# Four of the seven layer-0 tiles as three products of rounded parts and rests, and the diagonals on ScalarE

## The chip, the cores and the metric

The kernel runs on one core of a Trainium2 chip. The metric is the device time of one execution in microseconds (us), as the median of several runs. The core has five engines with queues of their own: TensorE (PE; its weight loads are shown apart, as PEld), VectorE (DVE), ScalarE (ACT), GpSimd (POOL) and SyncE (SP), which here only issues DMAs. The engines run their own instructions in order and wait for each other by semaphores.

## The reference

A recommendation tower: 39 embedding rows of 16 numbers for each of 512 samples, three layers of pairwise products with learned filters (a compressed interaction network), and three dense layers behind them.

```python
e = jnp.stack([tbl_f[ids[:, f]] for f in range(39)], axis=1)      # 512 x 39 x 16
x0 = xk = e
for W in (f0, f1, f2):                                            # 1521 x 128, 4992 x 128, 4992 x 128
    z = jnp.einsum('bfd,bgd->bfgd', x0, xk).reshape(b, f * g, d)
    cur = jnp.einsum('bpd,pm->bmd', z, W)                         # 512 x 128 x 16
    outs.append(cur); xk = cur
z = jnp.sum(jnp.concatenate(outs, axis=1), axis=-1)               # 512 x 384
h = jnp.maximum(jnp.concatenate([z, dense_ctx], axis=1) @ W_top1 + b_top1, 0.0)
h = jnp.maximum(h @ W_top2 + b_top2, 0.0)
y = h @ W_top3
```

## The kernel before

The batch is cut into 16 chunks of 32 samples, 512 columns (sample, dimension) each. Chunk 0 has its layer 0 in two halves; `i` counts these parts (part i is chunk i - 1 from i = 2 on).

Layer 0 of a part: because both factors are x0, pairs (f, g) are folded into 20 shifts, three shifts in a tile of 117 rows, seven tiles `t`. SyncE loads `x0_thrice` and, for each t, `shifted`; VectorE multiplies them into `z0` (`products0`, L525 to L538, the product at L537), which has three slots; TensorE multiplies z0 by `w0` in full fp32 and adds all seven tiles in the PSUM bank `acc0` (`layer0`, matmul at L755, two matmul records each). ScalarE then rounds acc0 to `x1_hi` (fp32r, `high_x1`, L631) and VectorE takes the rest `x1_lo` (`low_x1`, L545) and sums acc0 into `out0` (`sum_x1`, L550).

Layer 1 of a chunk: 40 strips (four sub-chunks `s` of 128 columns, ten strips `g` of up to four fields; the tenth has three). `layer1` makes each strip in three fp32r matmuls of up to 512 columns (L795 hi by hi, L796 hi by lo, L799 lo by hi) into one of seven PSUM banks. Each strip is scaled by x0 out of its bank: strips 0, 3, 5 and 8 of a sub-chunk by ScalarE (L687), strips 1, 2, 4, 6, 7 and 9 by VectorE (`scale`, L582, one instruction for a field). GpSimd adds ScalarE's products (L477) and VectorE's sums (L484, L487, L493) into `x2_t`, and between them issues the gathers of the embedding rows two chunks ahead (L467).

The order is written out by hand. Every engine walks the same loop over chunks c and places n = 0 to 39, one place for one strip, and the lists at the head of the file say at which place each other step stands; at a place these steps come ahead of the strip's own work. During chunk c, layer 0 of chunk c + 1 is made: `PRODUCT0_AT` has the places of VectorE's seven products, `LAYER0_AT` those of TensorE's seven tiles, `X1_AT` = (35, 36, 38) those of high_x1, low_x1 and sum_x1. The `_LATE_` lists hold for chunk 0 and for the chunks 4, 8 and 12, which close a quarter of the batch and carry layer 2 of that quarter (39 fp32 products, L827, at the places 13 to 20). TensorE turns x0 at place 6 (L764), and from chunk 1 on it makes at place 9 the sums of layer 2 of the chunk before (`sum_products`, L813), which take `x2_t` and the diagonals `x0_diag`. The diagonals are one VectorE instruction at place 20 (`diagonal`, L557).

The sums take four of the seven banks. The banks are handed out in turn, and a strip waits in `drained` until the slot seven before its own has been emptied. In a chunk from 1 on the strips 0 to 8 have the slots 0 to 8 of that chunk, the sums 9 to 12, strip 9 has 13, and strip 10 has 14. So the strip of place 9 waits for strip 6, that of place 10 for strip 7, that of place 11 for strip 8, and those from place 16 on for the strip seven before.

## Time and profile before

| what | value |
|---|---|
| median of 3 runs | 654.74 us (654.56 to 655.45) |
| the profiled execution | 655.72 us, of it 653.8 us span |
| PE busy | 623.2 us, 95% |
| PE weight loads busy | 468.0 us, 72% |
| DVE busy | 525.0 us, 80% |
| ACT busy | 337.7 us, 52% |
| POOL busy | 501.8 us, 77% |
| DMA engines, mean | 66 GB/s |
| chain that ended last, by engine | PE 90%, DMA 3%, DVE 2% |

The span is the time from the first to the last instruction in the trace; 1.9 us lie around it. Busy time is the time in which at least one instruction of an engine was under way, so instructions that overlap are counted once, while the mean duration of one counts each in full. Matmuls are pipelined: a 512-column matmul is recorded with 0.39 us, but in the chain of work the next one follows after 0.23 us, and that is its cost. The granted clock of TensorE is given as a share of full speed (2.4 GHz).

### The profile page before, as it was taken

The page shows a single profiled execution, that of the slowest core. Times are in us where ns is not written, and L with a number is a line of the kernel's source. Part 1 is how long each engine was busy: PE and PEld are TensorE (multiplying, and loading weights), DVE is VectorE, ACT ScalarE, POOL GpSimd, SP SyncE. Part 2 cuts the span into 40 slices and gives each one's busy share as a digit, 9 for nine tenths or more (in the row PEclk, how much of TensorE's full clock was granted, in tenths as well). Part 3 has the DMA queues.
Part 4 walks back from the last instruction along what each step waited for, and adds up shares of the span by engine and source line. Part 5 has one row for each costly group of instructions (what it writes and reads, how often), then busy time and mean ns, then how long its engine had stood idle before and what let it go on. Part 6 is the DMA issues. An engine that isn't in the chain of part 4 may idle for free.

```text
span 653.8 us, 10942 instructions
## 1 busy us (share of the span) xinstructions
PE 623.2 (95%) x3102; PEld 468.0 (72%) x3102; DVE 525.0 (80%) x1651; ACT 337.7 (52%) x1148; POOL 501.8 (77%) x486
## 2 busy tenths in 40 slices
PE   0599999999999999999999999999999999999998
PEld 0476777777796777777787777777787777778763
DVE  4499989989857898989867798989876798988800
ACT  3153646465543646565553556555553555557602
POOL 6789989898957889898975888898985786566710
PEclk9999999999999999999999999999999999999999
DMA  6464038231305013140404014040403104000000
GB/s 225 97 169 124 15 85 293 43 93 28 109 4 131 4 30 106 12 125 8 128 4 117 18 11 126 8 128 3 133 4 96 39 6 129 1 1 2 1 1 0
DMA packets 59014, 43.40 MB, mean 66 GB/s; under 512 B 37648, under 2 KB 42926, under 8 KB 58826
## 3 DMA queue, kind: packets, MB, share of 16 engines
q1 hardware_dynamic: 52854, 38.00, 20.0%
q0 software_dynamic: 5120, 1.32, 2.5%
q10 hardware_dynamic: 980, 3.39, 1.5%
q8 instruction: 24, 0.39, 0.3%
q14 instruction: 36, 0.29, 0.1%
HBM read 40.75 MB, written 1.94 MB: 65 GB/s over the span
## 4 chain that ended last, share of the span: by engine, by line
PE 90%; DMA 3%; DVE 2%; POOL 1%; SPq 1%; issue 1%; ACT 1%; POOLq 0%; DVEq 0%; ACTq 0%
PE strip L795 22%; PE strip L799 21%; PE strip L796 21%; PE acc L755 14%; PE acc L827 4%; PE strip L813 2%; DVE scaled L582 1%; PE strip L827 1%; PE strip L893 1%; PE acc L764 1%; DVE z L537 1%; DMA found<-in_tables,rows 1%; ACT first L687 1%; POOL found L467 1%; DMA shifted<-x_fields 0%
## 5 line engine op out<-in xcount | busy, mean ns | idle before, releaser
L582 DVE SCALAR_TENSOR_TENSOR scaled<-strip,x_t,scaled 128x128 f32<-128x128 f32 x1216 | 331.8, 340 | 26.8 <-PE strip L799 25.8
L795 PE MATMUL strip<-w_hi,x_hi 128*128 128x512 f32 (+1 forms) x640 | 298.3, 466 | 0.8 <-ACT x_hi L631 0.7
L799 PE MATMUL strip<-w_hi,x_lo 128*128 128x512 f32 (+1 forms) x640 | 248.9, 389 | 0.0
L796 PE MATMUL strip<-w_lo,x_hi 128*128 128x512 f32 (+1 forms) x640 | 248.4, 388 | 0.0
L477 POOL TENSOR_TENSOR added<-added,product 128x512 f32<-128x512 f32 x128 | 171.2, 1338 | 74.3 <-ACT product L687 71.3
L687 ACT ACTIVATE product<-strip,x_t 128x128 f32<-128x128 f32 x512 | 146.6, 372 | 144.1 <-PE strip L799 144.1
L467 POOL DMA_INDIRECT found<-in_tables,rows x160 | 160.7, 1004 | 28.5 <-issue 10.9
L795 PEld LDWEIGHTS strip<-w_hi,x_hi 128*128 128x128 f32 x640 | 120.2, 188 | 49.0 <-issue 15.0
L796 PEld LDWEIGHTS strip<-w_lo,x_hi 128*128 128x128 f32 x640 | 120.5, 188 | 44.9 <-issue 25.3
L799 PEld LDWEIGHTS strip<-w_hi,x_lo 128*128 128x128 f32 x640 | 120.1, 188 | 25.7
L687 ACT ACTIVATE added<-strip,x_t 128x128 f32<-128x128 f32 x256 | 73.0, 367 | 91.7 <-PE strip L799 91.7
L755 PE MATMUL acc<-z,w 117*128 117x512 f32 (+1 forms) x238 | 117.0, 577 | 3.2 <-ACT out L663 2.6
L582 DVE SCALAR_TENSOR_TENSOR scaled<-strip,x_t,first 128x128 f32<-128x128 f32 x256 | 71.8, 341 | 47.5 <-PE strip L799 25.0
L537 DVE TENSOR_TENSOR z<-shifted,x_thrice 117x512 f32<-117x512 f32 (+1 forms) x119 | 100.9, 850 | 10.9 <-DMA shifted<-x_half_fields 6.3
L484 POOL TENSOR_TENSOR added<-added,scaled 128x512 f32<-128x512 f32 x64 | 83.2, 1300 | 5.8 <-DVE scaled L582 2.9
L687 ACT ACTIVATE first<-strip,x_t 128x128 f32<-128x128 f32 x256 | 72.9, 367 | 27.5 <-PE strip L799 23.8
L755 PEld LDWEIGHTS acc<-z,w 117*128 117x128 f32 x238 | 45.1, 194 | 15.0 <-issue 4.3
L487 POOL TENSOR_TENSOR added<-added 128x256 f32<-128x256 f32 x64 | 51.4, 803 | 5.0
L493 POOL TENSOR_TENSOR x_t<-added 128x128 f32<-128x128 f32 x64 | 34.9, 545 | 5.0
L827 PEld LDWEIGHTS acc<-g_sum,w 128*128 128x128 f32 x234 | 29.8, 191 | 1.9
L827 PE MATMUL acc<-g_sum,w 128*128 128x128 f32 x234 | 30.0, 274 | 0.0
L654 ACT COPY g_sum<-strip 128x320 f32<-128x320 f32 (+2 forms) x68 | 24.4, 459 | 6.0 <-PE strip L813 6.0
(57 smaller groups left out, 181.7 us busy)
## 6 DMA issues: line engine op xcount, KB each, us to landing
shifted<-x_fields SPq DMA_DIRECT2D x105, 234.0 KB
x_thrice<-x_fields SPq DMA_DIRECT2D x15, 234.0 KB
found<-in_tables,rows POOLq DMA_INDIRECT x160, 5.0
w<-in_L_rec_f SPq DMA_DIRECT2D x1, 2496.0 KB, 10.4
g_sum<-in_L_rec_f ACTq DMA_DIRECT2D x4, 512.0 KB, 7.9
shifted<-x_half_fields SPq DMA_DIRECT2D x14, 117.0 KB
x_once<-x_fields SPq DMA_DIRECT2D x15, 78.0 KB
x_fields<-found SPq DMA_DIRECT2D x15, 72.0 KB
```

The source lines that it names most:

```text
L467: pool.indirect_dma_start(out=found[:, c % E_SLOTS, k, :], out_offset=None, in_=a["tables"][:, :], in_offset=bass.IndirectOffsetOnAxis(ap= ...
L477: pool.tensor_tensor(added[:, u % 2, :, :], added[:, u % 2, :, :], product[:, product_slot(u, k) % PRODUCTS, :, :], ALU.add).then_inc(add_ ...
L484: pool.tensor_tensor(added[:, u % 2, :, :], added[:, u % 2, :, :], scaled[:, u % 2, :, :], ALU.add).then_inc(add_step, 1)
L487: pool.tensor_tensor(added[:, u % 2, 0:2, :], added[:, u % 2, 0:2, :], added[:, u % 2, 2:4, :], ALU.add).then_inc(sum_step, 1)
L537: dve.tensor_tensor(z0[:, (T0 * i + t) % Z_SLOTS, columns], shifted[0:ROWS, t, columns], x0_thrice[:, p, columns], ALU.mult).then_inc(z0_r ...
L582: dve.scalar_tensor_tensor(into, strip[:, slot_of_strip(q) % Y_BANKS, j, :], x0_t[:, c % 2, s, f:f + 1], onto, ALU.mult, ALU.add).then_inc ...
L687: last = act.activation(into[:, j, :], strip[:, slot_of_strip(q) % Y_BANKS, j, :], ACT.Copy, scale=x0_t[:, c % 2, s, f:f + 1])
L755: pe.matmul(acc0[:, columns_of(i)], w0[:, t, :], z0[:, (T0 * i + t) % Z_SLOTS, columns_of(i)], start=(t == 0), stop=(t == T0 - 1)).then_in ...
L795: pe.matmul(into, x1_hi[:, c % 2, columns], hi, start=True, stop=False)
L796: pe.matmul(into, x1_hi[:, c % 2, columns], lo, start=False, stop=False)
L799: pe.matmul(into, x1_lo[:, c % 2, columns], hi, start=False, stop=True).then_inc(strip_ready, 1)
L827: last = pe.matmul(acc2[quarter], w2[:, f, :], g_sum[:, f, :], start=(f == 0), stop=(f == FIELDS - 1))
```

## The change

From chunk 2 on (parts i > 2, `in_three`), the last four tiles of layer 0 (t = 3 to 6) are no longer one fp32 product but three fp32r products: rounded w0 by rounded z0, rest of w0 by rounded z0, rounded w0 by rest of z0. The rounded part `z0_hi` is made by ScalarE (`high_z0`), the rest `z0_lo` by VectorE (`low_z0`); the parts of w0 are made once at the start. `z0` has a slot for each of its seven tiles instead of three in all. VectorE's products stand earlier: at the places 4, 5, 6, 7, 9, 11 and 13 instead of 6, 9, 12, 15, 18, 21 and 24, and in the late chunks at 8, 9, 10, 11, 13, 15 and 17 instead of 16 to 28; chunk 0 keeps its places. The rounded parts are made at 12, 14, 16 and 18, the rests at 13, 16, 19 and 22 (late: 16 to 22 and 18 to 27). The places of TensorE's tiles stay. The diagonals move from VectorE at place 20 to ScalarE at place 26, in two instructions instead of one. Left out below are only the declarations of the new tiles w0_hi and w0_lo and of the semaphores.

```diff
--- before.py
+++ after.py
@@ -105,7 +105,10 @@
 
 W1_PIECE = 8
 W1_PIECES = -(-FIELDS // W1_PIECE)
-Z_SLOTS = 3
+
+
+THREE = 4
+THREE_FROM = T0 - THREE
 
 
 
@@ -113,9 +116,14 @@
 DENSE_IN = 5
 DENSE_AT = 9
 KEEP_DENSE_AT = 10
-PRODUCT0_AT = [6, 9, 12, 15, 18, 21, 24]
+PRODUCT0_AT = [4, 5, 6, 7, 9, 11, 13]
+HIGH0_AT = [12, 14, 16, 18]
+LOW0_AT = [13, 16, 19, 22]
 LAYER0_AT = [12, 15, 18, 21, 24, 27, 30]
-PRODUCT0_LATE_AT = [16, 18, 20, 22, 24, 26, 28]
+PRODUCT0_FIRST_AT = [16, 18, 20, 22, 24, 26, 28]
+PRODUCT0_LATE_AT = [8, 9, 10, 11, 13, 15, 17]
+HIGH0_LATE_AT = [16, 18, 20, 22]
+LOW0_LATE_AT = [18, 21, 24, 27]
 LAYER0_LATE_AT = [22, 24, 26, 28, 30, 32, 34]
 TURN_X0_AT = (6, 8)
 X1_AT = (35, 36, 38)
@@ -125,7 +133,7 @@
 
 TURN_X0_LATE_AT = (17, 18)
 X1_HALF_AT = (13, 14, 15)
-DIAGONAL_AT = 20
+DIAGONAL_AT = 26
 LAYER2_AT = range(13, 21)
 LAYER2_STEP = 5
 KEEP_OUT1_AT = 12
@@ -170,6 +178,23 @@
     return c > 0 and c % PER_QUARTER == 0
 
 
+def in_three(i, t):
+
+    return i > HALVES and t >= THREE_FROM
+
+
+def three_before(i, t):
+    return THREE * (i - HALVES - 1) + t - THREE_FROM
+
+
+def parts0_at(c):
+
+    if c == 0 or c + 1 == CHUNKS:
+        return None, [], []
+    late = closes_quarter(c)
+    return part_of(c + 1, 0), HIGH0_LATE_AT if late else HIGH0_AT, LOW0_LATE_AT if late else LOW0_AT
+
+
 def layer0_at(c):
 
 
@@ -178,7 +203,8 @@
         plans.append((1, PRODUCT0_HALF_AT, LAYER0_HALF_AT, *TURN_X0_HALF_AT, *X1_HALF_AT))
     if c + 1 < CHUNKS:
         late = c == 0 or closes_quarter(c)
-        plans.append((part_of(c + 1, 0), PRODUCT0_LATE_AT if late else PRODUCT0_AT,
+        product_at = PRODUCT0_LATE_AT if c else PRODUCT0_FIRST_AT
+        plans.append((part_of(c + 1, 0), product_at if late else PRODUCT0_AT,
                       LAYER0_LATE_AT if late else LAYER0_AT,
                       *(TURN_X0_AT if c else TURN_X0_LATE_AT), *X1_AT))
     return plans
...
@@ -213,7 +241,9 @@
         x0_thrice = sb("x0_thrice", [ROWS, 2, N])
         x0_once = sb("x0_once", [P, 2, N])
         shifted = sb("shifted", [P, T0, N])
-        z0 = sb("z0", [ROWS, Z_SLOTS, N])
+        z0 = sb("z0", [ROWS, T0, N])
+        z0_hi = sb("z0_hi", [ROWS, THREE, N], F32R)
+        z0_lo = sb("z0_lo", [ROWS, THREE, N], F32R)
         x1_hi = sb("x1_hi", [MAPS, 2, N], F32R)
         x1_lo = sb("x1_lo", [MAPS, 2, N], F32R)
 
...
@@ -533,9 +567,21 @@
                     dve.wait_ge(thrice_in[p], 16 * arrivals(i))
                 dve.wait_ge(shifted_in[t], 16 * (i + 1))
 
-                at_least(dve, l0_step, T0 * i + t - Z_SLOTS + 1)
-                dve.tensor_tensor(z0[:, (T0 * i + t) % Z_SLOTS, columns], shifted[0:ROWS, t, columns],
+                if in_three(i - 1, t):
+                    dve.wait_ge(z0_lo_ready, three_before(i - 1, t) + 1)
+                else:
+                    at_least(dve, l0_step, T0 * (i - 1) + t + 1 if i else 0)
+                dve.tensor_tensor(z0[:, t, columns], shifted[0:ROWS, t, columns],
                                   x0_thrice[:, p, columns], ALU.mult).then_inc(z0_ready, 1)
+
+            def low_z0(i, t):
+                k = three_before(i, t)
+                dve.wait_ge(z0_hi_ready, k + 1)
+
+                if in_three(i - 1, t):
+                    dve.wait_ge(l0_step, T0 * (i - 1) + t + 1)
+                dve.tensor_tensor(z0_lo[:, t - THREE_FROM, :], z0[:, t, :], z0_hi[:, t - THREE_FROM, :].bitcast(F32),
+                                  ALU.subtract).then_inc(z0_lo_ready, 1)
 
             def low_x1(i):
                 p, columns = chunk_of(i) % 2, columns_of(i)
@@ -549,16 +595,6 @@
 
                 dve.tensor_reduce(out0[:, batch_of(i)], acc0[:, columns_of(i)].rearrange("m (b d) -> m b d", d=D),
                                   AX_X, ALU.add).then_inc(out0_ready, 1)
-
-            def diagonal(c):
-                dve.wait_ge(x0_t_ready, part_of(c, SUBS - 1) + 1)
-
-                at_least(dve, g_ready, c)
-                dve.tensor_tensor(
-                    x0_diag[:, :, :, 0:FIELDS],
-                    x0_t[:, c % 2, :, :].rearrange("p s (o f) -> p s o f", o=1).to_broadcast([P, SUBS, TILE_B, FIELDS]),
-                    mask[:].rearrange("p (a b o) -> p a b o", a=1, o=1).to_broadcast([P, SUBS, TILE_B, FIELDS]),
-                    ALU.mult).then_inc(diag_ready, 1)
 
             def scale(c, s, g):
 
@@ -592,6 +628,9 @@
                             .to_broadcast([P, SUBS, TILE_B])).then_inc(mask_set, 1)
             dve.wait_ge(w0_in, 32)
             dve.tensor_tensor(w0[:], w0[:], w0_mirror, ALU.add).then_inc(w0_ready, 1)
+            dve.wait_ge(w0_hi_ready, 1)
+            dve.tensor_tensor(w0_lo[:], w0[:, THREE_FROM:T0, :], w0_hi[:].bitcast(F32),
+                              ALU.subtract).then_inc(w0_lo_ready, 1)
 
             def low_w1(i):
                 of = w1_fields(i)
@@ -617,13 +656,31 @@
                             low_x1(i)
                         if n == sum_at:
                             sum_x1(i)
-                    if n == DIAGONAL_AT:
-                        diagonal(c)
+                    i, _, low_at = parts0_at(c)
+                    if n in low_at:
+                        low_z0(i, THREE_FROM + low_at.index(n))
                     if g in BY_DVE[s]:
                         scale(c, s, g)
 
         @block.scalar
         def _(act):
+            def high_z0(i, t):
+                act.wait_ge(z0_ready, T0 * i + t + 1)
+
+                if in_three(i - 1, t):
+                    act.wait_ge(l0_step, T0 * (i - 1) + t + 1)
+                act.copy(z0_hi[:, t - THREE_FROM, :], z0[:, t, :]).then_inc(z0_hi_ready, 1)
+
+            def diagonal(c):
+                act.wait_ge(x0_t_ready, part_of(c, SUBS - 1) + 1)
+                act.wait_ge(mask_in, 16)
+
+                at_least(act, g_ready, c)
+                for b in range(TILE_B):
+                    last = act.activation(x0_diag[:, :, b, 0:FIELDS], x0_t[:, c % 2, :, :], ACT.Copy,
+                                          scale=mask[:, b:b + 1])
+                last.then_inc(diag_ready, 1)
+
             def high_x1(i):
 
                 at_least(act, strip_ready, SLOTS * (chunk_of(i) - 1))
@@ -634,7 +691,6 @@
                 c, subs = chunk_of(i), subs_of(i)
 
                 at_least(act, scale_step, scaled_before(SUBS * (c - 1), 0) if c else 0)
-                at_least(act, diag_ready, c - 1)
                 act.wait_ge(x0_t_turned, i + 1)
                 act.copy(x0_t[:, c % 2, subs[0]:subs[-1] + 1, :],
                          x0_t_bank[i > 0][:, subs[0]:subs[-1] + 1, 0:FIELDS]).then_inc(x0_t_ready, 1)
@@ -694,6 +750,8 @@
             act.dma_start(w0_mirror, a["w0_lower"]).then_inc(w0_in, 16)
             for i in range(W1_PIECES):
                 act.dma_start(w1_raw[:, w1_fields(i), :], a["L0_rec_f1"][:, w1_fields(i), :]).then_inc(w1_in[i], 16)
+            act.wait_ge(w0_ready, 1)
+            act.copy(w0_hi[:], w0[:, THREE_FROM:T0, :]).then_inc(w0_hi_ready, 1)
             for i in range(W1_PIECES):
                 act.wait_ge(w1_in[i], 16)
                 act.copy(w1_hi[:, w1_fields(i), :], w1_raw[:, w1_fields(i), :]).then_inc(w1_hi_ready, 1)
@@ -714,6 +772,11 @@
                             high_x1(i)
                         if n == keep_at:
                             keep_x0_t(i)
+                    i, high_at, _ = parts0_at(c)
+                    if n in high_at:
+                        high_z0(i, THREE_FROM + high_at.index(n))
+                    if n == DIAGONAL_AT:
+                        diagonal(c)
                     if c and n == SUMS_AT:
                         keep_g(c - 1)
                     if c == CHUNKS - 1 and n == LAST_SUMS_AT:
@@ -741,7 +804,10 @@
         def _(pe):
             def layer0(i, t):
                 c = chunk_of(i)
-                pe.wait_ge(z0_ready, T0 * i + t + 1)
+                if in_three(i, t):
+                    pe.wait_ge(z0_lo_ready, three_before(i, t) + 1)
+                else:
+                    pe.wait_ge(z0_ready, T0 * i + t + 1)
                 if t == 0:
                     if i:
 
@@ -752,8 +818,15 @@
                     at_least(pe, out0_ready, i)
                     if closes_quarter(c - 1):
                         pe.wait_ge(out2_ready, (c - 1) // PER_QUARTER)
-                pe.matmul(acc0[:, columns_of(i)], w0[:, t, :], z0[:, (T0 * i + t) % Z_SLOTS, columns_of(i)],
-                          start=(t == 0), stop=(t == T0 - 1)).then_inc(l0_step, 1)
+                if in_three(i, t):
+                    k = t - THREE_FROM
+                    pe.matmul(acc0[:], w0_hi[:, k, :], z0_hi[:, k, :], start=False, stop=False)
+                    pe.matmul(acc0[:], w0_lo[:, k, :], z0_hi[:, k, :], start=False, stop=False)
+                    pe.matmul(acc0[:], w0_hi[:, k, :], z0_lo[:, k, :], start=False, stop=(t == T0 - 1)
+                              ).then_inc(l0_step, 1)
+                else:
+                    pe.matmul(acc0[:, columns_of(i)], w0[:, t, :], z0[:, t, columns_of(i)],
+                              start=(t == 0), stop=(t == T0 - 1)).then_inc(l0_step, 1)
 
             def turn_x0(i):
                 c = chunk_of(i)
@@ -835,6 +908,7 @@
             for t in range(T0):
                 layer0(0, t)
             pe.wait_ge(mask_set, 1)
+            pe.wait_ge(w0_lo_ready, 1)
             pe.wait_ge(x0_t_ready, 1)
 
             for c in range(CHUNKS):
```

## Rows read from the trace of the kernel before

**Rows 1.** Windows: span, PE, PEld, DVE, ACT, POOL busy (count); clock, DMA share, GB/s.
```profile
295.64:330.75 35.11, 35.11 (x175) 26.27 (x174) 32.71 (x105) 20.20 (x70) 31.26 (x31) 1.00 0.24 64
330.75:375.49 44.74, 43.87 (x252) 34.95 (x252) 31.24 (x103) 20.61 (x72) 30.89 (x31) 1.00 0.20 50
```

**Rows 2.** Chain of work that ended last, around place 9: start, duration, what.
```profile
295.64 1.06 PE strip L813 x32
296.70 0.38 PE strip L795
297.08 0.17 PE strip L796
297.25 0.18 PE strip L799
297.43 0.41 PE strip L795
297.84 0.23 PE strip L796
...
299.00 0.86 PE acc L755 x2
```

**Rows 3.** Waits between 74 and 600 us: total, times, longest.
```profile
PEld strip L795 <- DVE scaled L582: 12.7, 52, 0.4
```

**Rows 4.** Timeline of VectorE ahead of that place: start, duration, instruction, count.
```profile
292.42 2.15 DVE L582 SCALAR_TENSOR_TENSOR scaled<-strip,x_t,scaled 128x128 f32<-128x128 f32 x8
294.48 0.73 DVE L537 TENSOR_TENSOR z<-shifted,x_thrice 117x512 f32<-117x512 f32 x1
295.14 2.15 DVE L582 SCALAR_TENSOR_TENSOR scaled<-strip,x_t,scaled 128x128 f32<-128x128 f32 x8
297.21 2.14 DVE L537 TENSOR_TENSOR z<-shifted,x_thrice 117x512 f32<-117x512 f32 x1
299.28 0.86 DVE L582 SCALAR_TENSOR_TENSOR scaled<-strip,x_t,scaled 128x128 f32<-128x128 f32 x3
```

**Rows 5.** Groups of instructions by shape: busy, mean ns of one | idle before.
```profile
L537 DVE TENSOR_TENSOR z<-shifted,x_thrice 117x512 f32<-117x512 f32 x105 | 95.2, 907 | 3.6 <-PE acc L755 3.5
L557 DVE TENSOR_TENSOR x_diag<-x_t,mask 128x312 f32<-128x312 f32 x16 | 16.6, 1037 | 0.0
L631 ACT CAST x_hi<-acc 128x512 fp32r<-128x512 f32 x15 | 9.0, 602 | 0.1
```

**Rows 6.** Timeline of GpSimd over the same stretch.
```profile
293.39 0.74 POOL L487 TENSOR_TENSOR added<-added 128x256 f32<-128x256 f32 x1
294.21 0.46 POOL L493 TENSOR_TENSOR x_t<-added 128x128 f32<-128x128 f32 x1
294.62 1.74 POOL L477 TENSOR_TENSOR added<-added,product 128x512 f32<-128x512 f32 x1
296.51 0.96 POOL L467 DMA_INDIRECT found<-in_tables,rows  x1
297.49 1.31 POOL L477 TENSOR_TENSOR added<-added,product 128x512 f32<-128x512 f32 x1
```

**Rows 7.** Timeline of VectorE at the end of the chunk (idle before in brackets).
```profile
319.34 1.13 DVE L582 SCALAR_TENSOR_TENSOR scaled<-strip,x_t,first 128x128 f32<-128x128 f32 x4 [2.11 <-PE strip L799]
```

**Rows 8.** First chunk after a late one: VectorE's product at place 9, TensorE's chain.
```profile
225.97 0.68 DVE L537 TENSOR_TENSOR z<-shifted,x_thrice 117x512 f32<-117x512 f32 x1
226.27 0.38 PE strip L795
376.69 0.68 DVE L537 TENSOR_TENSOR z<-shifted,x_thrice 117x512 f32<-117x512 f32 x1
376.55 0.38 PE strip L795
```

**Rows 9.** Chain of work in part 0 and chunk 0.
```profile
26.64 0.42 DVE z L537
52.74 0.39 DVE x_diag L557
```

**Rows 10.** DMA queue of SyncE: last loads of one part, in the chunk ahead of its products.
```profile
313.58 5.80 SPq L420 DMA_DIRECT2D shifted<-x_fields  x7
```

**Rows 11.** TensorE idle near the end (idle before in brackets), and that window.
```profile
623.17 0.46 PE L813 MATMUL strip<-x_diag,x_t 32*128 32x80 f32 x8 [1.50 <-POOL x_t L493]
619.00:626.00 7.00, 5.50 (x31) 3.06 (x30) 0.14 (x1) 1.02 (x6) 3.70 (x4) 1.00 0.01 2
```

More of the change, by code:

```diff
@@ L204, in build_program @@
         w0 = sb("w0", [ROWS, T0, MAPS])
+        w0_hi = sb("w0_hi", [ROWS, THREE, MAPS], F32R)
+        w0_lo = sb("w0_lo", [ROWS, THREE, MAPS], F32R)
         w1_hi = sb("w1_hi", [P, FIELDS, MAPS], F32R)
@@ L281, in build_program @@
         w0_ready = sem("w0_ready")
+        w0_hi_ready = sem("w0_hi_ready")
+        w0_lo_ready = sem("w0_lo_ready")
         w1_hi_ready = sem("w1_hi_ready")
@@ L288, in build_program @@
         z0_ready = sem("z0_ready")
+        z0_hi_ready = sem("z0_hi_ready")
+        z0_lo_ready = sem("z0_lo_ready")
         l0_step = sem("l0_step")
```

## The prediction

> **What bounds the kernel now.** I read the views in this order: busy time in windows from one place 9 to the next, the chain of work that ended last, the waits, and then the timelines of the two engines that meet where the chain has its only irregular pieces.
>
> An ordinary chunk takes 35.11 us, and TensorE is busy for all of it; VectorE is busy for 32.71 us, so it has 2.4 us to spare, GpSimd 31.26 and ScalarE 20.20 us [rows 1]. A chunk that closes a quarter takes 44.74 us with VectorE at 31.24. TensorE sets the pace, and whatever shortens its own work shortens the chunk, as long as nobody makes it wait. That is where the reader should look twice. In the chain around place 9 the pieces of 512 columns follow each other every 0.23 us, but the first matmul of the strip at place 10 stands with 0.41 us [rows 2]: 0.18 us of waiting. The cause is VectorE: strip 10 may only start when the bank of strip 7 is empty, and VectorE ends strip 7 at 297.21, where its next instruction starts, 0.22 us before TensorE starts strip 10 at 297.43 [rows 2, 4]. The same piece, 0.36 to 0.48 us long, stands in 8 of the 11 ordinary chunks from chunk 1 to 14 (chunks 1, 2, 3, 6, 7, 10, 11, 14); in all, weight loads of strips waited for VectorE 52 times, most of them hidden behind the running matmul [rows 3]. So at the end of strip 7 VectorE has no slack, although it has 2.4 us over the whole chunk. Four of seven banks go to the sums at place 9, and the lead of TensorE over VectorE shrinks to three strips there.
>
> **TensorE's products.** An fp32 tile costs 0.86 us in the chain, an fp32r matmul of 512 columns 0.23 (three of them, from 297.84 on, take 0.70) [rows 2]. Per tile 0.86 - 0.70 = 0.16 us are saved; four tiles in 14 parts make 56 tiles, 56 x 0.163 = 9.1 us. Weight loads go from two to three a tile and fit under a matmul, as those of the strips do. TensorE never waits longer for z0_lo: a rest stands at least seven places ahead of its tile (13 to 21, 16 to 24, 19 to 27, 22 to 30; late 18 to 28 down to 27 to 34), and TensorE can't be more than seven strips ahead of VectorE.
>
> [...]
>
> **VectorE over the chunk.** Added are four rests a chunk, the same shape and the same two SBUF inputs as a product. A product has a mean of 0.907 us, 0.83 without the 0.08 in which neighbours overlap; removed is the diagonal, 1.04 - 0.08 = 0.96 [rows 5]. Per ordinary chunk 4 x 0.83 - 0.96 = +2.4 us, so VectorE needs some 32.8 + 2.4 = 35.2 us: about the old length of the chunk, just above the new length of TensorE's work (35.11 - 0.65 = 34.5).
>
> **VectorE up to strip 7: the step that decides.** Before, one product (place 6) stood ahead of the scaling of strip 7. Now four do: places 4, 5, 6 and 7, and strips 4, 6 and 7 are scaled between them. Strips 9 and 10 of TensorE wait for strips 6 and 7, so the three added products fall on the path. What each costs depends on GpSimd. Where GpSimd is in one of its additions, the product ends some 0.5 us after it: the product at 297.21 took 2.14 us, to 299.28, because the addition from 297.49 lasted to 298.80 [rows 4, 6]; undisturbed it takes 0.60 (0.68 recorded).
>
> I walk VectorE in the chunk of rows 4. Strips 2 and 4 take 2.06 us, so strip 2 ends at 293.45. Product 0 finds L487 running until 294.13 and ends at 294.60; strip 4 ends at 295.63; product 1 finds L477, shifted to about 295.2 to 296.5, and ends at 296.97; product 2 meets the gather, which doesn't hold it, and ends at 297.57; strip 6 at 298.60; product 3 finds the second L477 and ends at 299.42; strip 7 at 300.45. That is 3.2 us later than 297.21. If GpSimd's chain comes 0.6 us earlier (it has more time in a longer chunk), the same walk gives 299.8, 2.6 us later. With no conflict at all it is 293.45 + 4 x 0.60 + 3 x 1.03 = 298.94, 1.7 us later; with all four products held, about 3.8. I take S = 2.8 between the two walks, with ends 1.7 and 3.8.
>
> Nothing absorbs it. VectorE's lag when it enters the chunk is set behind its idle time near place 31 (2.11 us ahead of that strip) [rows 7]: from there on it has low_x1, sum_x1 and six strips at their unchanged places. After strip 7 it has three products, four rests and its strips up to place 29, and by the same walk it catches up with TensorE there, with 1 to 2 us idle, because a chunk now lasts 35.1 - 0.65 + 2.8 = 37.3 us against 35.2 us of its work. So the stall comes anew in every ordinary chunk.
>
> In the first chunk after a late one there is slack: VectorE ends strip 7 at 225.97, and TensorE would start strip 10 at 226.27 + 0.73 = 227.00, so 0.8 us are free in chunk 5 (after the 0.22 of latency); by the same reckoning 0.4 at 376.69 and in chunk 13 [rows 8]. Sum of stalls: 8 x 2.8 + (2.8 - 0.8) + 2 x (2.8 - 0.4) = 29.2 us. In the late chunks the products start at place 8, behind strip 7, and layer 2 gives VectorE time: no stall, the 0.65 us are kept.
>
> The Trainium skill (SBUF — State Buffer, SBUF: two separate sides) says that VectorE with two SBUF inputs and GpSimd exclude each other for a whole instruction, and that whichever starts first gets the ports. The first half agrees with the 2.14 us; the second doesn't, since the product is recorded 0.28 us ahead of the addition that held it. By that half, products recorded first would all take 0.60; in my walk the three that are held meet a running addition, so it would leave S as it is.
>
> **What costs nothing.** ScalarE gets four roundings of at most 0.60 us (the mean of x_hi) [rows 5] and two diagonal pieces of about 0.3: 3.0 us on 20.20 of 35.11 [rows 1]. They stand at the places 12 to 18 and 26, ahead of strips for which TensorE is late; nobody but VectorE's rests waits for them, and these come later in VectorE's queue. If that cover were gone it would be 3.0 us a chunk. SyncE: the loads of a part are issued by 313.58 + 5.80 = 319.4, in the chunk ahead, about 9 us before the new place 4 [rows 10]. Each load waits for the product of the part before, which comes earlier now. The start: seven z0 slots free the product at 26.64, which waited for TensorE, and the diagonal of 0.39 leaves the path in chunk 0 [rows 9]; -0.6 us, between 0 and -0.9. The new preparation of w0 falls where VectorE and ScalarE wait for loads. The tail is unchanged.
>
> **Sum.** -9.1 + 29.2 - 0.6 = +19.5 us on the profiled 655.72 gives 675.2. The median of the runs lies 0.98 lower: 654.74 + 19.5 = 674.2 us.
>
> **The rivals.**
> - The wait at place 10 is covered, because VectorE enters the chunk early enough and its whole work becomes the bound: the ordinary chunks take 35.2 us (+0.1 x 11), the late ones save 0.65 x 3, the start 0.6: -1.5 us, 653.3. Against it: the lag at entry can shrink by at most the 0.9 us for which strip 1 lies ready. Chance 0.05.
> - Faster: the wait is covered and VectorE keeps up as well, products near 0.60. Then -9.1 - 0.6 gives 645.0. It decides when four products before strip 7 cost no more than the one does now, for which the timeline has no room. Chance 0.07.
> - More than the forecast: all products and rests are held by GpSimd, ScalarE is late with strips after its roundings, or TensorE's clock falls in the gaps. TensorE would stand for up to 2 us at strip 9 and 1.4 us at strip 10; at 623.17 it was idle for 1.50 us and the clock stayed at 1.00 (2.4 GHz) [rows 11]. At S = 3.8 plus 1 us for each ordinary chunk: 8 x 3.8 + 3.0 + 6.8 + 11 - 9.7 = +41.5, 696. Chance 0.12.
> - The change doesn't do what it says: three fp32r products as long as the fp32 one. Then nothing is saved and the time is 683; the same form costs 0.23 in the strips. It is inside the range.
>
> **How the numbers follow.** The forecast has 0.76. Its own ends are S = 1.7 (13.6 + 0.9 + 2.6 - 9.1 - 0.9 = +7.1, 662) and S = 3.8 (30.4 + 3.0 + 6.8 - 9.1 = +31.1, 686). The range 661 to 687 leaves out the first two rivals and most of the third. A measurement tells about 0.2% from no change: faster 0.07, same 0.05, slower 0.88.
>
> **What the profile would show.** Right: in ordinary chunks the chain has gaps of 1 to 2 us on TensorE at the first matmuls of the strips at places 9 and 10, put down to VectorE's scaling, ordinary chunks near 37 us, late chunks near 44.1, three matmuls of 0.23 for the tiles from place 21 on, VectorE idle for 1 to 2 us near place 30. Wrong: ordinary chunks of 34.5 us (the pinch was not one), or idle time of TensorE elsewhere, as ahead of the tiles (waiting for z0_lo) or of strips that ScalarE should have emptied.

## The result, and the profile after

The changed kernel takes 705.55 us (704.32 to 707.3, 4 runs) against 655.10 beside it: a ratio of 1.0764, 95% interval 1.0747 to 1.0782. It is slower by 50 us, where 19.5 were forecast; the time lies above the range (661 to 687). The profiled execution has a span of 705.5 us with a mean granted clock of 0.954 (before 653.8 and 1.000).

First the windows of the changed kernel, cut at the starts of the sums at place 9, the columns as in [rows 1]: two ordinary chunks and a late one.

```profile
115.11:155.83 40.72, 36.93 (x175) 28.42 (x174) 35.28 (x106) 22.79 (x76) 31.79 (x31) 0.92 0.29 75
320.17:360.79 40.62, 36.95 (x175) 28.31 (x174) 35.28 (x109) 22.79 (x76) 31.82 (x31) 0.92 0.22 55
360.79:404.90 44.11, 43.24 (x253) 35.74 (x253) 33.46 (x104) 23.27 (x78) 32.37 (x31) 1.00 0.20 51
```

Chunk 8, the late one, does what the sum said: 44.11 for 44.74, 0.63 us less. The ordinary ones take 5.5 us more, TensorE is idle for 3.8 us of them, and its clock is below one. From start to start of the sums, all chunks:

| chunk | 1 | 2 | 3 | 4 late | 5 | 6 | 7 | 8 late | 9 | 10 | 11 | 12 late | 13 | 14 |
|---|---|---|---|---|---|---|---|---|---|---|---|---|---|---|
| before | 35.31 | 35.13 | 35.12 | 45.17 | 35.31 | 35.13 | 35.11 | 44.74 | 34.92 | 35.08 | 35.18 | 44.73 | 34.93 | 34.61 |
| after | 40.64 | 40.72 | 40.84 | 44.82 | 38.29 | 40.39 | 40.62 | 44.11 | 39.15 | 40.17 | 40.53 | 44.10 | 38.54 | 39.16 |

The eleven ordinary chunks cost 53.2 us more, the late ones give 1.6 back (0.35 in chunk 4, 0.63 in each of the others); the first sums start at 74.47 instead of 74.40, so the start gained nothing. That is the whole difference of the spans, 51.7 us.

Now the place that answers to [rows 2] and [rows 4]. TensorE's timeline from the sums of chunk 2 on, with the idle time before an instruction in brackets:

```profile
115.11 1.13 PE L886 MATMUL strip<-x_diag,x_t 32*128 32x80 f32 x32
118.14 0.45 PE L868 MATMUL strip<-w_hi,x_hi 128*128 128x384 f32 x1 [1.89 <-DVE scaled L618]
...
120.83 0.80 PE L868 MATMUL strip<-w_hi,x_hi 128*128 128x512 f32 x1 [1.90 <-DVE scaled L618]
```

The two gaps stand where they were expected, ahead of the strips of places 9 and 10, and both wait for VectorE's scaling. Strip 10 starts 5.72 us after the sums; before it was 1.78 (109.71 to 111.49 in the same chunk). So S, the delay that the prediction put at 2.8 us, is 3.94. VectorE over this stretch (L574 is the product, L618 the scaling):

```profile
112.99 0.69 DVE L574 TENSOR_TENSOR z<-shifted,x_thrice 117x512 f32<-117x512 f32 x1
113.61 1.11 DVE L618 SCALAR_TENSOR_TENSOR scaled<-strip,x_t,scaled 128x128 f32<-128x128 f32 x4
114.65 2.40 DVE L574 TENSOR_TENSOR z<-shifted,x_thrice 117x512 f32<-117x512 f32 x2
116.97 1.11 DVE L618 SCALAR_TENSOR_TENSOR scaled<-strip,x_t,scaled 128x128 f32<-128x128 f32 x4
118.01 1.73 DVE L574 TENSOR_TENSOR z<-shifted,x_thrice 117x512 f32<-117x512 f32 x1
119.67 1.11 DVE L618 SCALAR_TENSOR_TENSOR scaled<-strip,x_t,scaled 128x128 f32<-128x128 f32 x4
```

Four products, three scalings, in the order of the walk; from the end of strip 2 (112.99) to that of strip 7 (120.70) it is 7.7 us, where the walk had 7.0. The four products take 4.6 us of it, undisturbed they would take 4 x 0.60. GpSimd beside it, which answers to [rows 6]:

```profile
113.22 1.07 POOL L521 TENSOR_TENSOR added<-added 128x256 f32<-128x256 f32 x1
114.37 0.46 POOL L527 TENSOR_TENSOR x_t<-added 128x128 f32<-128x128 f32 x1
114.79 1.72 POOL L511 TENSOR_TENSOR added<-added,product 128x512 f32<-128x512 f32 x1
116.65 1.23 POOL L501 DMA_INDIRECT found<-in_tables,rows  x1
117.91 1.28 POOL L511 TENSOR_TENSOR added<-added,product 128x512 f32<-128x512 f32 x1
```

The first product was not held: it starts 0.23 us ahead of the addition at 113.22, ends in time, and the addition takes 1.07 us instead of 0.74. So GpSimd is held too, and its gather beside product 2 takes 1.23 us instead of 0.96. With a start that is 0.36 later against the sums, this brings its second long addition 0.95 us later than before (2.80 us after the start of the sums, before 1.85). That addition starts 0.1 us ahead of product 3 and holds it to the end: the product takes 1.66 us, where the walk had 0.82. The walk had too much for the first product, too little for the last, and too little by 0.7 us in all.

Then the chain of work behind the second gap:

```profile
120.83 0.80 PE strip L868
121.63 0.43 PE strip L869
122.06 0.43 PE strip L872
122.48 0.43 PE strip L868
122.91 0.43 PE strip L869
123.34 0.43 PE strip L872
123.76 1.71 PE acc L828 x2
125.47 0.41 PE strip L868
125.88 0.24 PE strip L869
```

A matmul of 512 columns takes 0.43 us here instead of 0.23, the fp32 tile 1.71 instead of 0.86 [rows 2], until 125.88. The windows before, in and behind it show the clock: TensorE worked 1.93 of 5.72 us, and the granted clock of the next five is 0.51, the lower of its two levels (1.2 GHz), then full again (2.4 GHz).

```profile
115.11:120.83 5.72, 1.93 (x36) 1.46 (x35) 5.72 (x12) 2.46 (x8) 5.13 (x4) 0.83 0.56 146
120.83:125.83 5.00, 5.00 (x10) 3.32 (x11) 3.05 (x9) 1.65 (x5) 3.22 (x4) 0.51 0.02 2
125.83:132.83 7.00, 7.00 (x30) 5.12 (x29) 6.45 (x20) 4.32 (x13) 2.58 (x3) 1.00 0.01 1
```

The pieces from 120.83 to 125.88 last 5.05 us; at full clock they are 7 x 0.233 + 0.86 = 2.5. The difference is 2.5 us; 0.1 to 0.2 of it, an estimate, is the usual longer first piece behind a wait (0.18 in [rows 2]), so the clock takes some 2.4 us. Sum for the chunk: 3.94 + 2.4 - 0.65 = 5.7, measured 5.59.

### The profile page after: what moved, and what is told of

The parts are those of the page before. It is cut to its first block, busy times and chain, and to the rows that moved or that the text cites. A ratio compares the mean times of both kernels' runs of the same rounds, so it can differ in the third digit from the quotient of the medians.

```text
span 705.5 us, 11285 instructions
## 1 busy us (share of the span) xinstructions
PE 640.1 (91%) x3158; PEld 493.6 (70%) x3158; DVE 558.1 (79%) x1692; ACT 376.3 (53%) x1237; POOL 508.2 (72%) x486
## 4 chain that ended last, share of the span: by engine, by line
PE 76%; DVE 12%; issue 6%; DMA 2%; POOL 1%; SPq 1%; ACT 1%; DVEq 0%; POOLq 0%; ACTq 0%
PE strip L868 19%; PE strip L872 18%; PE strip L869 18%; DVE scaled L618 9%; PE acc L828 8%; PE acc L900 4%; DVE z L574 3%; PE acc L823 2%; PE acc L824 2%; PE acc L825 2%; PE strip L900 1%; PE strip L967 1%; PE strip L886 1%; ACT first L743 1%; DMA found<-in_tables,rows 1%
## 5 line engine op out<-in xcount | busy, mean ns | idle before, releaser
L618 DVE SCALAR_TENSOR_TENSOR scaled<-strip,x_t,scaled 128x128 f32<-128x128 f32 x1216 | 332.3, 339 | 33.2 <-PE strip L872 32.4
L868 PE MATMUL strip<-w_hi,x_hi 128*128 128x512 f32 (+1 forms) x640 | 285.9, 447 | 35.3 <-DVE scaled L618 34.6
L872 PE MATMUL strip<-w_hi,x_lo 128*128 128x512 f32 (+1 forms) x640 | 255.1, 399 | 0.0
L869 PE MATMUL strip<-w_lo,x_hi 128*128 128x512 f32 (+1 forms) x640 | 254.9, 398 | 0.0
L501 POOL DMA_INDIRECT found<-in_tables,rows x160 | 165.9, 1037 | 28.8 <-issue 12.7
L868 PEld LDWEIGHTS strip<-w_hi,x_hi 128*128 128x128 f32 x640 | 124.3, 194 | 78.8 <-DVE scaled L618 45.9
L869 PEld LDWEIGHTS strip<-w_lo,x_hi 128*128 128x128 f32 x640 | 124.6, 195 | 35.9 <-issue 13.5
L618 DVE SCALAR_TENSOR_TENSOR scaled<-strip,x_t,first 128x128 f32<-128x128 f32 x256 | 71.9, 343 | 63.8 <-PE strip L872 48.2
L574 DVE TENSOR_TENSOR z<-shifted,x_thrice 117x512 f32<-117x512 f32 (+1 forms) x119 | 103.8, 885 | 7.6 <-DMA shifted<-x_half_fields 7.6
L828 PE MATMUL acc<-z,w 117*128 117x512 f32 (+1 forms) x126 | 66.8, 624 | 3.3 <-ACT out L719 2.9
L583 DVE TENSOR_TENSOR z_lo<-z,z_hi 117x512 fp32r<-117x512 f32 x56 | 48.1, 859 | 0.0
L828 PEld LDWEIGHTS acc<-z,w 117*128 117x128 f32 x126 | 27.7, 226 | 12.3 <-issue 4.1
L672 ACT CAST z_hi<-z 117x512 fp32r<-117x512 f32 x56 | 34.0, 638 | 0.0
```

What stands on the lines that cost most here:

```text
L501: pool.indirect_dma_start(out=found[:, c % E_SLOTS, k, :], out_offset=None, in_=a["tables"][:, :], in_offset=bass.IndirectOffsetOnAxis(ap= ...
L574: dve.tensor_tensor(z0[:, t, columns], shifted[0:ROWS, t, columns], x0_thrice[:, p, columns], ALU.mult).then_inc(z0_ready, 1)
L618: dve.scalar_tensor_tensor(into, strip[:, slot_of_strip(q) % Y_BANKS, j, :], x0_t[:, c % 2, s, f:f + 1], onto, ALU.mult, ALU.add).then_inc ...
L828: pe.matmul(acc0[:, columns_of(i)], w0[:, t, :], z0[:, t, columns_of(i)], start=(t == 0), stop=(t == T0 - 1)).then_inc(l0_step, 1)
L868: pe.matmul(into, x1_hi[:, c % 2, columns], hi, start=True, stop=False)
L869: pe.matmul(into, x1_hi[:, c % 2, columns], lo, start=False, stop=False)
```

## The experiments

Theory A: the products ahead of strip 7 make TensorE wait, and the idle time drops its clock. Rivals: VectorE's longer work over the whole chunk (B), and ScalarE's roundings (C). Where a run is compared by chunks, their length is again that from sums to sums.

### The places of the products alone

```diff
-Z_SLOTS = 3
+Z_SLOTS = 7
-PRODUCT0_AT = [6, 9, 12, 15, 18, 21, 24]
+PRODUCT0_AT = [4, 5, 6, 7, 9, 11, 13]
```

> The kernel before, with seven slots for z0 and VectorE's products of ordinary chunks at the new places 4, 5, 6, 7, 9, 11, 13; no rounded parts, no rests, the diagonal stays on VectorE, the late chunks as before. Theory A (the four products ahead of strip 7 make TensorE wait at strips 9 and 10, and its clock then halves for some us): the whole loss is here, without the gain of 0.65 us a chunk: 654.7 + 51.7 + 9.1 = 715 us, ordinary chunks near 41.2 us. Theory B (the rests, VectorE's longer work over the chunk, are what costs): 655 to 660 us. Theory C (the roundings on ScalarE make strips late): 655 to 660 us as well.

Measured 704.24 us (703.94 to 704.53), ratio 1.0749 (1.0727 to 1.0770). The loss is there without a single rest or rounding: B and C fall as its cause. It is 11 us below what A gave; some 7.5 of them lie in four chunks in which the clock didn't fall, 1.8 in chunk 1, whose gaps are shorter (1.3 us each). Two chunks of this run:

```profile
278.70:319.33 40.63, 36.85 (x172) 27.32 (x171) 32.67 (x103) 20.18 (x70) 32.04 (x31) 0.96 0.21 55
404.85:442.67 37.82, 35.27 (x172) 26.27 (x171) 31.36 (x103) 20.19 (x70) 31.04 (x31) 1.00 0.24 60
```

The second is chunk 9, the first after a late one, with gaps of 1.25 and 1.31 us: the clock stayed up. In chunks 5, 13 and 14 it did as well. In the changed kernel it fell in all eleven, behind gaps of nearly the same lengths in these four. What decides between the two is open.

### One product ahead of strip 7

```diff
-PRODUCT0_AT = [4, 5, 6, 7, 9, 11, 13]      -LAYER0_AT = [12, 15, 18, 21, 24, 27, 30]
+PRODUCT0_AT = [6, 9, 11, 12, 14, 16, 18]   +LAYER0_AT = [12, 15, 18, 24, 27, 30, 33]
-HIGH0_AT = [12, 14, 16, 18]                -LOW0_AT = [13, 16, 19, 22]
+HIGH0_AT = [15, 17, 19, 21]                +LOW0_AT = [16, 19, 22, 25]
```

> The changed kernel with one product ahead of strip 7 instead of four: products at 6, 9, 11, 12, 14, 16, 18, roundings at 15, 17, 19, 21, rests at 16, 19, 22, 25, tiles 3 to 6 of TensorE at 24, 27, 30, 33. All work of the change is in it. Theory A: no long gaps and no fall of the clock; ordinary chunks at 34.5 us if VectorE keeps up, 35.2 if its whole work sets them: 646 to 654 us, I expect 650. Theory B: VectorE's added work costs wherever it stands: over 665 us. Theory C: ScalarE's work is the same as in the changed kernel, so over 665 us.

Measured 660.54 us (659.09 to 661.31), ratio 1.0078 (1.0061 to 1.0095), clock 1.00. All the work of the change costs 5 us when it isn't bunched ahead of strip 7; 45 of the 50 us were its place. But the 9 us that TensorE saves don't show, and A's 650 was wrong. An ordinary chunk, and TensorE at its start:

```profile
299.04:334.65 35.61, 35.11 (x175) 26.66 (x175) 35.59 (x106) 22.64 (x76) 31.63 (x31) 1.00 0.25 63
...
299.04 1.13 PE L886 MATMUL strip<-x_diag,x_t 32*128 32x80 f32 x32 [0.91 <-POOL x_t L527]
```

VectorE is busy for 35.59 of 35.61 us, and TensorE waits at the sums for GpSimd's last addition: there is a second bound behind the first. It is followed below.

### The gaps filled

```diff
+                    if c and c + 1 < CHUNKS and not closes_quarter(c) and c != DENSE_IN and n in (9, 10):
+                        pe.wait_ge(x0_t_ready, part_of(c + 1, 0) + 1)
+                        for _ in range(7):
+                            pe.matmul(acc0[:], w1_hi[:, 0, :], x1_hi[:, c % 2, :], start=True, stop=True)
                     layer1(c, s, g)
```

> The changed kernel, with seven throwaway matmuls of 512 columns (1.6 us at full clock) on TensorE ahead of each of the strips 9 and 10 of ordinary chunks, except in chunk 5; their result is overwritten by the next layer 0. TensorE works through most of the two gaps of 1.9 us. Theory A: the gaps stay as long, the clock doesn't fall behind them, and some 2.4 us in each of ten chunks come back: near 682 us, granted clock 1.00. If the slow matmuls behind the gaps have another cause than the idle time: 705 us or more.

Measured 685.92 us (685.65 to 686.61), ratio 1.0472 (1.0455 to 1.0490), clock 1.00. More work on TensorE, 19.6 us less. Chunk 2 of it starts its fillers at 112.40 and 115.02:

```profile
112.40 1.89 PE L940 MATMUL acc<-x_hi,w_hi 128*128 128x512 f32 x7
114.39 0.44 PE L869 MATMUL strip<-w_hi,x_hi 128*128 128x384 f32 x1
```

The chunks 2, 3, 6, 7, 10 and 11 take 38.4 to 38.6 us where the changed kernel has 40.2 to 40.8: the clock is 1.6 to 2.4 us a chunk, 2.05 in the mean, and the rest, 38.45 - 35.12 + 0.65 = 4.0, is the waiting. In these six chunks strip 10 starts as late as in the changed kernel, within 0.03 us. So they hold the waiting fixed and take the clock away, and the split is measured and not only argued. In the chunks 9, 13 and 14 the fillers themselves make strip 10 0.5 to 0.6 us later. Chunk 5 got no fillers and has the same two gaps as in the changed kernel (0.81 and 1.3 us); here the clock stayed up behind them, and it takes 1.4 us less.

### GpSimd's additions cut short

```diff
-pool.tensor_tensor(added[:, u % 2, :, :], added[:, u % 2, :, :], ...      (L477, L484, L487 alike)
+pool.tensor_tensor(added[:, u % 2, :, 0:16], added[:, u % 2, :, 0:16], ...
```

> The changed kernel with three of GpSimd's four additions on 16 of 128 columns of each field (the sums of layer 2 are then not the reference's). GpSimd hardly ever works while VectorE multiplies. Theory A with the conflict as second factor: a product costs 0.60 us, strip 7 ends 1.7 us later than in the kernel before instead of 3.9, the two gaps are under 1 us each; if the clock then stays up, ordinary chunks take 35.1 - 0.65 + 1.7 = 36.2 us and the whole 663 us; if it falls all the same, 688 us. If the conflict with GpSimd has no part in it: 705 us.

The kernel leaves out 112 of the 128 columns in three of GpSimd's four additions. Measured 674.49 us (673.56 to 675.42), ratio 1.0295 (1.0274 to 1.0315). Strip 10 starts 3.51 us after the sums: S = 1.74, the conflict-free end of the range. So of S = 3.94 GpSimd's additions make 2.2 us. The gaps are 0.75 and 0.84 us, and still the clock fell in eight of eleven chunks. Chunk 10, where it stayed, chunk 11, where it didn't, and five us behind the gap of chunk 11:

```profile
423.17:459.41 36.24, 34.65 (x176) 27.01 (x175) 32.17 (x106) 22.83 (x76) 17.35 (x31) 1.00 0.24 62
459.41:497.21 37.80, 36.21 (x175) 28.07 (x174) 32.25 (x109) 22.82 (x76) 17.35 (x31) 0.95 0.22 60
...
462.92:467.92 5.00, 5.00 (x13) 3.56 (x14) 3.22 (x10) 1.65 (x5) 2.30 (x4) 0.66 0.04 3
```

Chunk 10 is as calculated (36.2). The two have the same gaps and differ by 1.56 us, the price of one fall.

### Two products ahead of strip 7

```diff
-PRODUCT0_AT = [4, 5, 6, 7, 9, 11, 13]
+PRODUCT0_AT = [4, 6, 8, 9, 10, 11, 13]
```

> The changed kernel with two products ahead of strip 7 instead of four (places 4, 6, 8, 9, 10, 11, 13); all else as changed. Theory A: one added product before strip 7 makes it 0.6 to 1.7 us late, one gap of about 1 us at strip 10. Ordinary chunks 35.1 - 0.65 + 1.2 = 35.7 us if the clock stays, and some 1.6 us more in those where it falls: 662 us with none, 680 with all. The theory that only the amount of VectorE's work counts: 705 as the changed kernel, which has the same work.

Measured 669.46 us (669.04 to 669.89), ratio 1.0217 (1.0191 to 1.0242), 9 us above the run with one product ahead. Strip 10 comes 0.4 to 1.2 us later than in the kernel before in ten of the eleven chunks. But the gaps ahead of the strips 9 and 10 are short (up to 0.78 and 0.24 us), and no clock fell behind them. It fell in the chunks 3, 7 and 11, behind another wait, at the sums:

```profile
149.23 1.13 PE L886 MATMUL strip<-x_diag,x_t 32*128 32x80 f32 x32 [1.83 <-POOL x_t L527]
```

GpSimd's last addition of the chunks 2, 6 and 10 comes 1.83 us late. These three chunks take 38.1 us and hold 6 of the 8.5 us between this profile and that of the run with one product ahead. So theory A had the time about right (662 to 680) and the place only in part.

### The second bound: two and three tiles

```diff
-THREE = 4
+THREE = 2     (or 3; THREE_FROM = T0 - THREE; fewer entries in the lists of roundings and rests)
```

> Only the last two tiles of layer 0 in three products, products at 6, 9, 11, 12, 14, 15, 17, roundings at 17 and 19, rests at 19 and 22, TensorE's tiles at their old places (27 and 30 for these two). VectorE has two rests and no diagonal: 32.8 - 0.96 + 2 x 0.9 = 33.6 us a chunk. If VectorE's whole work sets the chunk of the run with four rests (35.6 to 36.1 us), two are below TensorE's 35.12 - 0.33 = 34.8, and the kernel takes 655.3 - 4.6 = 650.7 us. If something else of the change costs (the places of the products, ScalarE's queue): 658 us or more.

> As the kernel with two tiles in three products, and no product at all ahead of strip 7 (places 8, 9, 11, 12, 14, 15, 17). Theory A: the 0.18 us that TensorE waited for strip 7 in eight chunks go too, 1.4 us in all: 649.3 us. If TensorE then waits at place 12 for the product made at place 8, or the 0.18 us weren't VectorE's: 650.7 us or more.

> The last three tiles in three products, no product ahead of strip 7 (places 8, 9, 11, 12, 13, 15, 17), roundings at 15, 17, 19, rests at 17, 19, 22. TensorE's work is 35.12 - 0.49 = 34.6 us a chunk, VectorE's 32.8 - 0.96 + 3 x 0.9 = 34.5. If VectorE's work is the second bound, this is where the two meet: 648 to 653 us, ordinary chunks of 34.6 to 35.2, between the four-rest run and the two-rest run and not much better than two. If it isn't: 647 us.

Measured 655.62, 655.45 and 655.32 us, ratios 1.0007 (0.9993 to 1.0021), 0.9997 (0.9987 to 1.0007) and 0.9997 (0.9983 to 1.0010). All three take the time of the kernel before, whatever TensorE saves. It is a sum that cancels: the late chunks and the chunks 1, 5, 13 and 14 are shorter, while in the seven others TensorE waits 0.2 to 1.3 us at the sums for GpSimd's last addition, and they take 34.9 to 35.9 us instead of 34.9 to 35.2. Two rests or three make no difference to the time, so the expectation that the amount of VectorE's work is the second bound fell. The chain of the run with three tiles, ahead of the sums of chunk 8:

```profile
326.86 0.96 POOL found L501
...
327.85 1.30 POOL added L511
...
329.22 1.29 POOL added L518
...
330.59 0.73 POOL added L521
...
331.39 0.46 POOL x_t L527
...
331.89 1.11 PE strip L886 x29
```

Its last 5 us run through GpSimd (ahead of 326.86 it runs over VectorE's scalings), and TensorE waits at place 9 for the last addition. In this run GpSimd works from 308.60 to these sums with no wait over 0.16 us. The 31.3 busy us of 35.1 in [rows 1] leave out the pauses of about 0.1 us between its instructions, so they looked like more room than there was.

### GpSimd relieved

The short additions once more, in the run with one product ahead of strip 7 and four tiles, and in the kernel before:

> The run with four tiles in three products and one product ahead of strip 7 (660.5 us), with three of GpSimd's four additions on 16 of 128 columns of each field (the sums of layer 2 are then not the reference's). In the runs with two and three tiles TensorE waited at place 9 for GpSimd's last addition of the chunk before, and both stayed at 655.4 us. Theory D (GpSimd's chain of additions and gathers is the second bound, 35.3 us a chunk and more): TensorE's whole saving shows, ordinary chunks at 34.5 us, the kernel at 655.4 - 9.1 = 646.3 us. If VectorE's own work were the second bound: 35.2 us a chunk or more, 654 us and more.

> The kernel before with the same short additions (the sums of layer 2 are then not the reference's). There GpSimd isn't late and TensorE sets the pace: 653 to 655 us, at most the 0.18 us of eight chunks and some at the end of the last chunk (2 us of GpSimd's additions there) less. Should it be far lower, GpSimd was a bound of the kernel before already.

Measured 642.67 us (ratio 0.9803, 0.9781 to 0.9825) and 652.96 (ratio 0.9964, 0.9950 to 0.9977). With GpSimd out of the way the change saves 10.3 us: the forecast 9.1 and the small waits for strip 7, which the kernel before keeps with short additions too (0.14 us in eight chunks).

A chunk of the run with four tiles:

```profile
290.45:324.70 34.25, 34.25 (x176) 27.05 (x175) 32.01 (x107) 22.78 (x76) 19.07 (x31) 1.00 0.25 65
```

TensorE is busy for the whole 34.25 us. VectorE has the same instructions as in the window of 35.61 us above and needs 32.0: its 35.59 there held 3.6 us of waiting for GpSimd. The kernel before gains only 2.5 us, most of it behind the last chunk. So the second bound is the pair that hold each other, and GpSimd's chain ends last: that TensorE waits for it at the sums is in the traces, but the short additions relieve both engines at once, and how much of the bound is GpSimd's own work and how much the holding is not separated.

### A strip taken from ScalarE, so that GpSimd adds less

```diff
-BY_ACT = ((0, 3, 5, 8),) * SUBS
+BY_ACT = ((0, 3, 5, 8),) * (SUBS - 1) + ((0, 3, 7),)      (or (0, 3, 7) in the second sub-chunk)
```

> The run with two tiles in three products and no product ahead of strip 7 (655.4 us), with one strip of the last sub-chunk given from ScalarE to VectorE (ScalarE has 0, 3, 7 there), so that GpSimd has one addition of 1.3 us less a chunk. Theory D: GpSimd's chain falls to 35.3 - 1.4 = 33.9 us, VectorE's work rises by four scalings to 33.6 + 1.0 = 34.6, TensorE's 34.8 us set the chunk: 650.9 us. If GpSimd isn't the bound: 655 us or more.

> The same, with the strip given away in the second sub-chunk (places 10 to 19) instead of the last. Theory D: the chain is as much shorter, 650.9 us; but VectorE has its products and rests at the places 8 to 22 and gets its four scalings there as well, so TensorE may wait there for a bank, 651 to 655 us. It tells whether the place of the relief matters or only its amount.

Measured 658.58 us (ratio 1.0047, 1.0032 to 1.0062) and 677.83 (1.0330, 1.0301 to 1.0360), both above the 650.9 expected. In the first most ordinary chunks take 35.6 us, the first sums start 1.9 us later than in the kernel before, and TensorE waits 0.2 us at the sums for VectorE's scaling instead of for GpSimd; in the second TensorE waits up to 3.2 us for GpSimd's last addition and its clock falls. Theory D's bound gave way in the first run, as it said, but the strip couldn't be moved for a gain: with four more scalings VectorE ends last, at 34.6 busy us of 35.6. In the second run GpSimd's additions come later, not earlier; why was not followed.

### The late chunks alone, and the diagonals alone

```diff
-    return i > HALVES and t >= THREE_FROM
+    return i > HALVES and closes_quarter(chunk_of(i) - 1) and t >= THREE_FROM
```

> Three products only for the four last tiles made in the chunks 4, 8 and 12; ordinary chunks as in the kernel before (products at 6, 9, 12, 15, 18, 21, 24), with the diagonals on ScalarE. If only the other engines' load hid the gain: 3 x 0.65 = 1.9 us less, 653.5 us. If the parts cost something themselves: 655.4 us or more.

> The same with all seven tiles of the chunks 4, 8 and 12 in three products: 3 x 7 x 0.163 = 3.4 us less, 652.0 us, late chunks near 43.6 us; 655.4 us or more if the parts cost something themselves.

> The kernel before with the diagonals on ScalarE at place 26 and nothing else changed. TensorE sets the pace of the chunks, so VectorE's 1 us less a chunk changes nothing there; 0.4 us less in chunk 0: 655.0 us. If VectorE's relief moved strip 7 earlier, the 0.18 us of eight chunks would go too: 653.6 us.

Measured 655.72 us (ratio 0.9997, 0.9987 to 1.0008), 655.90 (0.9990, 0.9974 to 1.0006) and 656.28 (1.0016, 1.0004 to 1.0029). In the profiles of the first two the late chunks take 0.63 us less each with four tiles and 1.1 us with seven, as calculated. But the first sums start at 75.26 and 76.72 us instead of 74.40, and chunk 6 of the first and chunk 1 of the second are 1.3 and 1.2 us longer. The diagonals on ScalarE gain nothing by themselves.

The single executions tell more than the medians. All executions of the kernel before have a mean clock of 1.000. With seven tiles five of twelve have 1.000 and take 653.02 to 653.86 us; the other seven have 0.995 to 0.997 and take 655.87 to 657.77. The profile is of one of these: TensorE waits 2.72 us for GpSimd's last addition ahead of the first sums, and over the next five us its clock is 0.66. With the diagonals alone it is the same picture: seven executions at 1.000 (654.97 to 656.40 us), five at 0.997 (657.07 to 658.73). So with seven tiles the gain of 2.5 us is there where the clock stays up, and one fall of the clock takes it.

A last run took seven tiles in the late chunks and left the ordinary chunks, the diagonals and the pace of the start as before:

> All seven tiles of the chunks 4, 8 and 12 in three products, as in the run before, but the diagonals back on VectorE at place 20 and, up to part 2, VectorE's products held to TensorE's pace as with three slots, so that the start runs as in the kernel before. In the run with the diagonals on ScalarE the three late chunks took 1.1 us less each, while the start reached the first sums of layer 2 up to 2.3 us later and used the gain up. If the moved diagonals and the freed products of the start are what delays it: 655.9 - 3.3 = 652.6 us and the first sums at 74.4 us. If the start varies for another reason: between 653 and 656.5, as there.

Measured 653.30 us (652.16 to 656.71, 12 runs) against 655.96: ratio 0.9976, 0.9959 to 0.9993. It is below the kernel before by 0.24%. Its first sums start at 74.80 us, and its late chunks hold the gain:

```profile
479.16:522.79 43.63, 42.76 (x266) 36.28 (x260) 35.84 (x110) 24.02 (x81) 33.29 (x30) 1.00 0.19 52
```

The twelve executions fall into two groups again: eight with a mean clock of 1.000 take 652.16 to 653.45 us, as much less as expected (652.6), and four with 0.997 take 656.35 to 656.71. Against five and seven before, the numbers are too small to say that the diagonals or the start made the difference. That the fall stands at the first sums is shown in one profile, that of seven tiles with the diagonals on ScalarE; in the others it is likely.

## Why the prediction went as it did

**The bound and the place: right.** TensorE set the pace, strip 7 was where VectorE had no slack, and the three added products fell on the path in each ordinary chunk, less after a late one (S = 2.3 to 2.8 us in the chunks 5, 9 and 13). The gaps stand at strips 9 and 10.

**TensorE's saving: right in size, wrong as a free term.** 0.63 us in two of the three late chunks, 10.3 us in the run with short additions. In most ordinary chunks it couldn't have shown even without the stall: once the products stood behind strip 7, TensorE waited for GpSimd, and these chunks took 34.9 to 36.1 us. The prediction read GpSimd's 31.26 us of busy time as room and had no rival in which it ends last.

**S: mis-sized.** 2.8 us, measured 3.94, just outside its ends (1.7 and 3.8). The lower end was exact (1.74 without the additions). The term that failed is the conflict: (2.8 - 1.7) / 4 = 0.28 us for each of four products, measured (3.94 - 1.74) / 4 = 0.55. The case "GpSimd comes earlier" didn't happen; it comes later, because products hold its additions and gathers as well, and so the last product meets the whole of an addition. The rule of the walk, taken from the product at 297.21 alone, was also too simple: that product began while a gather was running, and products that began like this mostly lost against an addition behind them, while those that began beside nothing held it (counts below).

**The clock: the larger miss.** It was named in the third rival, with idle time of 1.50 us at 623.17 as evidence that it would hold [rows 11], and priced at no more than 1 us a chunk together with two other mishaps. It costs 1.6 to 2.4 us in ordinary chunks, some 20 us in all (the run with filled gaps). The step that failed is the reading of one gap: a single one with TensorE busy on both sides says little about two gaps in 5.7 us with 1.9 us of work. It is also what puts the time outside the range. With S = 3.94 and the clock free the prediction's own sum gives 8 x 3.94 + (3.94 - 0.8) + 2 x (3.94 - 0.4) - 9.1 - 0.6 = +32.0 us, 686.8, just inside. With 11 x 2.05 for the clock it is +54.6, where the spans differ by 51.7; the chunks 5, 9, 13 and 14, whose gaps were shorter, took 4.4 us less than this sum gives them, the others a little more.

**VectorE over the chunk.** The catch-up near place 30 was right. 35.2 us for its whole work agrees with the changed kernel (35.28) and is neither the 35.59 with one product ahead of strip 7 nor the 32.0 with short additions: it isn't a property of VectorE's queue alone.

**The start.** -0.6 us was expected, +0.07 measured, but this term can't be judged by one profile: over all the runs the first sums start between 73.6 and 76.7 us. The roundings on ScalarE took 0.64 us each and the two pieces of a diagonal 0.44 each, where 0.60 and 0.3 were assumed; TensorE didn't wait for them in the windows above, and the places alone, without them, lose as much.

## What to carry to other kernels

Look for slack at the point where the buffers are fewest, not over the stage: VectorE had 2.4 us in the chunk and none at strip 7. Price a wait of TensorE with its clock: here a gap could be followed by up to five us at half speed, so 4 us of waiting cost 6. When moving work off the bounding engine, cut the next engine's work short in a trial first, to see whether there is anything to win. And look at the single executions beside their median: where they fall into groups with different clocks, the median says how often the clock fell, not what the change is worth.

## What the runs showed of the hardware

- TensorE's clock fell to its lower level behind gaps of 0.75 and 0.84 us in some chunks and stayed up behind 1.25 and 1.31 us in others; the same gaps do both, at a price of 1.4 to 2.4 us for a fall. It also fell behind a single wait of 1.83 us at the sums (the run with two products ahead) and stayed up behind one of 1.50 us near the end [rows 11].
- Throwaway matmuls in a gap paid for themselves: 140 added, 19.6 us less.
- A VectorE product with two SBUF inputs and a GpSimd addition hold each other both ways: 0.60 us became up to 2.1, and 0.74 became 1.07.
- Who is held depends on more than the order. In the kernel before, 8 products of 117 x 512 began up to 0.5 us ahead of an addition with GpSimd otherwise idle: all 8 took 0.7 us, and the addition took 0.2 to 0.5 us longer. Another 11 began so while a gather was still running: 8 of them, recorded 0.16 to 0.28 us ahead of the addition, took 2.0 to 2.1 us and ended behind it; 3, recorded 0.28 to 0.29 us ahead, took 0.7.
- A gather alone doesn't hold a product (0.67 to 0.68 recorded in all 32 products of 512 columns that met only a gather in the kernel before). The product can hold the gather: in the changed kernel, from the first sums on, 29 of the 50 gathers beside a product or a rest took over 1.1 us, of the 74 others none (0.96 in the middle).
- ScalarE's rounding of 117 x 512 out of SBUF takes 0.64 us; the two pieces of a diagonal 0.44 each.
